# A sparse-attention loop: weighing and sum copy behind both pairs of heads of the next step

## What is computed

```
q, k, v = proj(Wq), proj(Wk), proj(Wv)         # 16 heads of 8, L = 1024, 32 blocks of 32
compressed_out = attn(q, mean of k per block, mean of v per block)
_, idx = top_k(block_scores, 8)                 # 8 blocks per head
selected_out = attn(q, k[idx], v[idx])          # the same 256 keys for all queries of a head
sliding_out  = attn(q, k, v, mask=(j <= i) & (j > i - 128))
out = g0 * compressed_out + g1 * selected_out + g2 * sliding_out
x = x + out @ Wo + bo
```

## Time and profile before

| what | value |
|---|---|
| time, median of three runs | 3937.93 us (3936.81 to 3938.05) |
| profiled execution, span | 3917.3 us, 87847 instructions |
| PE busy in the span | 3234.5 us (83%) |
| DVE busy | 2819.6 us (72%) |
| ACT busy | 2311.6 us (59%) |
| POOL busy | 1236.0 us (32%) |
| mean granted TensorE clock | 0.878 |

### The profile page before, as it was taken

One profiled execution on the slowest core, in us unless ns is written; L12 is line 12 of the kernel. 1 busy time (PEld: TensorE's weight loads), 2 busy tenths in 40 slices (PEclk: granted clock), 3 DMA queues, 4 the chain that ended last, 5 costly groups with the idle time before them and its releaser, 6 DMA issues. The chain is left out here.

```text
span 3917.3 us, 87847 instructions
## 1 busy us (share of the span) xinstructions
PE 3234.5 (83%) x36196; PEld 1484.2 (38%) x36256; DVE 2819.6 (72%) x4293; ACT 2311.6 (59%) x3868; POOL 1236.0 (32%) x1018
## 2 busy tenths in 40 slices
PE   6999999899867767699988888887995676776799
PEld 1222222266511121156533333333453554554445
DVE  8898899587679999887746667755535667656643
ACT  3888888766554555266532566665645564543565
POOL 1100100055537778545533000001004665452100
PEclk7999999899968788799999999998997676756799
DMA  4101010100010010100045011101000000000100
GB/s 102 28 9 28 20 21 5 37 2 2 11 32 17 17 33 17 35 15 2 13 71 76 10 38 32 27 21 53 1 9 3 4 4 4 4 4 3 31 7 17
DMA packets 136019, 84.34 MB, mean 22 GB/s; under 512 B 92386, under 2 KB 107539, under 8 KB 135491
## 3 DMA queue, kind: packets, MB, share of 16 engines
q1 hardware_dynamic: 132870, 74.45, 8.8%
q0 software_dynamic: 2688, 4.20, 0.7%
q10 hardware_dynamic: 64, 0.07, 0.0%
HBM read 46.97 MB, written 18.33 MB: 17 GB/s over the span
## 5 line engine op out<-in xcount | busy, mean ns | idle before, releaser
L993 DVE TENSOR_REDUCE attn_peak_halves<-attn_ps 128x2 f32<-128x1024 f32 x512 | 601.4, 1218 | 54.8 <-PE attn_ps L824 47.1
L946 ACT ACTIVATE attn_weights<-attn_ps 128x512 f32<-128x512 f32 x1024 | 531.1, 601 | 97.3 <-PE attn_ps L852 97.2
L2991 DVE TENSOR_REDUCE sparse_peak<-sparse_ps 128x4 f32<-128x1024 f32 x256 | 309.6, 1223 | 136.2 <-PE sparse_ps L2617 134.5
L1254 POOL TENSOR_TENSOR moe_hidden<-moe_exact,moe_hidden 128x512 f16<-128x512 f32 x256 | 296.7, 1163 | 331.9 <-ACT moe_hidden L1238 323.4
L3693 POOL TENSOR_TENSOR delta_q<-delta_q,delta_weighted 128x512 f32<-128x512 f32 x240 | 322.2, 1369 | 238.8 <-ACT delta_weighted L4087 238.7
L2844 ACT ACTIVATE sparse_weights<-sparse_ps 128x512 f32<-128x512 f32 (+1 forms) x512 | 272.0, 585 | 173.6 <-PE sparse_ps L2684 87.9
L250 PE MATMUL moe_ps<-moe_xT_halves,moe_w_halves 128*128 128x512 f16 x1536 | 364.0, 384 | 9.3 <-DVE moe_w_halves L1271 5.9
L1789 POOL TENSOR_TENSOR mamba_out_c<-mamba_states,mamba_c_rep 128x1024 f32<-128x1024 f32 x128 | 301.4, 2366 | 167.9 <-DVE mamba_states L1856 136.7
L852 PE MATMUL attn_ps<-attn_q_stack,attn_k_stack 50*128 50x512 f16 x1024 | 321.2, 385 | 27.0 <-ACT attn_weights L946 7.1
L250 PE MATMUL ffn_ps<-ffn_layers,ffn_h_halves 128*128 128x512 f16 x1536 | 334.5, 379 | 3.5 <-ACT ffn_gate L3236 3.5
L1575 PE MATMUL mamba_ps<-mamba_stack,mamba_spread 96*128 96x512 bf16 x512 | 194.0, 482 | 138.8 <-DVE mamba_states L1856 78.3
(11 more groups left out here) (450 smaller groups left out, 6280.9 us busy)
## 6 DMA issues: line engine op xcount, KB each, us to landing
mamba_stack<-mamba_parts SPq DMA_DIRECT2D x96, 128.0 KB, 2.4
sparse_factor<-sp_factor SPq DMA_DIRECT2D x24, 256.0 KB
sp_halves<-sparse_parts SPq DMA_DIRECT2D x8, 512.0 KB, 3.1
ffn_h<-in_h SPq DMA_DIRECT2D x4, 1024.0 KB, 7.8
attn_q_stack<-attn_halves SPq DMA_DIRECT2D x96, 32.0 KB
attn_k_stack<-attn_halves SPq DMA_DIRECT2D x96, 32.0 KB
attn_halves<-attn_hp SPq DMA_DIRECT2D x8, 384.0 KB, 3.1
attn_q_stack<-attn_peak_rows SPq DMA_DIRECT2D x128, 2.0 KB
```

What stands on the lines that cost most here:

```text
L946: act.activation(weights[:, at % 2, h, :], use.slot, ACT.Exp).then_inc(*key_act.one())
L993: dve.tensor_reduce(peak_halves[:, turn % PEAKS, keys, at:at + 2], use.slot, AX_X, ALU.max).then_inc(*score_dve.one())
L1254: pool.tensor_tensor(low, exact_sb[:, i % 3, :], hidden[:, i // EB % 3, i % EB, 0, :], ALU.subtract).then_inc(*hidden_low.one())
L2991: dve.tensor_reduce(peak[:, at % PEAKS, unit // 2, 4 * r:4 * r + 4], use.slot.rearrange("p h (a k) -> p (h a) k", a=2), AX_X, ALU.max).the ...
```

## The change

In each step the weighing of the step before stood between the first pair and the second, and the copy of its sum behind the second. Now both stand behind the second pair. The ten products of `warm` move with the weighing. Nothing else is changed: the calls are the same, and so is their number.

```diff
@@ -2215,10 +2215,11 @@
                             yield "exp", g, half, s, h
                         yield "pair", g, half, s, pair
                         yield from next_score()
-                        if g % GROUPS < 2 and n == 5 and pair == 0:
-                            yield ("warm", 10, *pending)
-                        if pending:
-                            yield ("sum" if pair else "weigh", *pending)
+                    if g % GROUPS < 2 and n == 5:
+                        yield ("warm", 10, *pending)
+                    if pending:
+                        yield ("weigh", *pending)
+                        yield ("sum", *pending)
                     pending = (g, half, s)
                     yield from between(g, n)
```

## The result

| | before | after |
|---|---|---|
| median, same chip (5 executions each) | 3937.93 us | 3915.49 us |
| lowest, highest | 3929.33, 3938.18 | 3910.77, 3920.11 |
| ratio | | 0.9949, 95% interval 0.9937 to 0.9962 |
| span of the profiled execution | 3917.3 | 3916.9 |
| its own time | not given | 3918.72 |

The change makes the kernel faster by 20 us (3937.93 x 0.0051), with an interval of 15 to 25.

What follows compares the result with a forecast made beforehand. Loop bound by a chain hopping between engines, mostly on TensorE. Terms 10.4 - 2 + 2.5 + 1 + 2 + 1 = 14.9 us take the span 3917.3 to 3902.4; plus 20.6, 3923, range 3908 to 3936.

Steps and rivals of the forecast that it cites:

- first steps: Loop's first steps: DVE's block scores hold TensorE up in some six places, the weighing moves into such waits; 1 us gained.
- numerators: Behind the second pair of s=1, seven times: they no longer hide an open exponential; 0.3 each, 2 us lost.
- last three halves: Halves without scores: 1.0 us saved at the wait for POOL, 2 us on six steps with a copy.
- Regular halves: Loop halves with scores: two take 25.92 us against 26.64, 0.36 saved a half, 10.4 us over 29 halves.
- open wait at s=1: Step s=1: the second pair waits for exponential 1 too, a new wait of 0.6 to 0.8 us.
- sign of being wrong: Regular steps s=3: the forecast is wrong if they do not shorten by some 0.15 us in the mean.
- Projections: Six in the loop: idle ahead falls from 2.4 to about 1.4 us, some may keep full clock; 2.5 us gained.
- Dummies: Ten dummy products of 8 steps: they stand before the weighing either way, their time is the same; costed at nothing.
- The 20.6: Whole kernel: timed median lies 20.6 us above the profiled span, for what is around it; carried over to the forecast.
- Waits only change place: Loop steps: later exponentials and 0.1 us longer handover per step take 11.6 of the 14.9 us back; 3935, chance 0.20.
- Slower, the clock falls at the wait of s=1: Loop halves: clock falls to 1.2 GHz once per half, 28 us net loss, 3966; slower cases together chance 0.09.
- The clock stays up: Projections and tail: the higher clock level holds after all of them; 24 to 28 us gained, 3912, chance 0.13.

Runs made afterwards that it cites:

- s3_only: Changed kernel, but weighing behind both pairs only in steps s=3, elsewhere and the dummies between the pairs as before; 3923.04 us, ratio 0.9966 to the kernel before.
- all_but_s3: Changed kernel, but in steps s=3 the weighing is between the pairs as before; 3934.63 us, ratio 1.0001 to the kernel before.
- before_filled: Kernel before the change with three dummy products added ahead of each of the six projections; 3933.86 us, ratio 0.9989 to the kernel before.
- s0_s3: Changed kernel, but weighing between the pairs at s=1 and s=2, behind both at s=0 and s=3, dummies between; 3896.14 us, ratio 0.9904 to the kernel before.
- warm_stays: Changed kernel with only the ten dummy products put back between the pairs; 3911.56 us, ratio 0.9940 to the kernel before.
- exit_swap: Changed kernel with the last half's inversion and factor store listed ahead of the previous half's projection after the loop; 3912.98 us, ratio 0.9947 to the kernel before.
- s1_back: Changed kernel with weighing and dummy products between the pairs again in steps s=1 only; 3898.78 us, ratio 0.9909 to the kernel before.
- before_again: The kernel before the change, unaltered, run and profiled once more; 3934.01 us, ratio 1.0002 to the kernel before.
- after_again: The changed kernel, unaltered, run and profiled once more; 3916.26 us, ratio 0.9948 to the kernel before.

## Why the prediction was right, and where it was not

My terms, put to the same four pieces (in us gained):

| piece | predicted | measured |
|---|---|---|
| first two halves: 0.7 of order, 1 of first steps | 1.7 | 1.4 |
| 27 halves: order 9.7, numerators -2, clock 2.5 | 10.2 | 10.1 |
| last three halves: 1 + 2 | 3 | 8.4 |
| exit | 0 | -2.9 |
| sum | 14.9 | 17.0 |

- **Regular halves, 25.92 for two.** Measured 25.98, so 0.33 a half and 8.9 for the 27. The waits for the copy went; the open wait at s=1 came at its place and in its size (0.6 to 0.8 said, 0.67 seen). s=1 is 3.35 (3.45 said), s=3 3.52 (3.48). One sign of being wrong was that the steps s=3 don't shorten by some 0.15 in the mean: they shorten by 0.12 (3.39 became 3.52 in a first half, 3.88 became 3.52 in a second), so the sign stands just short of its mark. s3_only shows that the move at s=3 brings the gain, as the prediction had it. That the cause is the wait for the copy is supported by 31 waits gone and not isolated: all_but_s3 has lost these waits too.
- **Numerators, 2 lost.** Their 384-wide step went from 4.79 to 4.92 where the plain one went from 3.30 to 3.20, 0.23 each; the 512-wide one went from 5.00 to 5.24 where the plain one went from 3.46 to 3.53, 0.17 each. That is 1.2 for the six in the 27 halves and 1.4 for all seven. Right.
- **Projections.** Idle 1.4 said, 1.43 and 1.64 found. The clock's term was 2.5. Set against the same steps at full clock (6.00, or 8.38 with dummies, in before_filled; 3.20 for the plain step behind), those of before were too long by 7.5 in sum. Those of after were too long by 4.4: twice 1.26 up to the second pair, and 0.90 and 0.96 in the step behind, whose dummies ran slower (6.69 and 6.75 instead of 5.79). So 3.1 was gained. before_filled, with the order of all else kept, gains 4.6 by three projections. Order 8.9, numerators -1.2, clock 3.1 and dummies -0.6 (2.26 instead of 2.17, seven times) make 10.2 of the measured 10.1.
- **Last three halves, 3.** This is the term that was mis-sized most. The scores run out two halves before the end, not three: DVE is busy 9.72 of the 13.65 us up to 2621.70 and 2.54 of the 35.9 behind. So 0.6 of the 8.4 is one more regular second half, and 7.8 is made in the last two. There TensorE's busy time fell by 5.2 (27.36 to 22.15), with the clock going from 0.76 to 1.00. Other kernels have three of the steps of before in the same order and at full clock. Two of them, before and then in s3_only, by their second pairs:
```profile
2644.95 0.61 PE L2664 MATMUL sparse_ps<-sparse_q_stack,sparse_p_stack 28*128 28x512 f16 x2
...
2651.47 0.39 PE L2684 MATMUL sparse_ps<-sparse_q_stack,sparse_k_stack 28*128 28x256 f16 x6
```
```profile
2633.38 0.39 PE L2670 MATMUL sparse_ps<-sparse_q_stack,sparse_p_stack 28*128 28x512 f16 x2
...
2637.93 0.39 PE L2690 MATMUL sparse_ps<-sparse_q_stack,sparse_k_stack 28*128 28x256 f16 x6
```
The step between them, which has numerators in it, took 6.52 before and 4.55 there; the step ahead of it 3.96 and 3.11; and the first step s=2 of the last two halves 4.74, and 3.02 in s0_s3. These three are 4.5 us of clock. The order and all else have at most 3.3 of the 7.8, and I had 3. I priced the order and forgot the clock, though the profile shows 0.76 there before. What raised it is open: warm_stays has the order of after there, and in it the lower level did come once (a step of 6.59 instead of 5.01).
- **Exit.** Not reckoned; 2.9 lost, shown by exit_swap. I followed the loop to its last pair and not the lists of the engines behind it.
- **Dummies, "at nothing".** Against before that is right within 0.7. But "their time is the same" (2.17 and 2.26 in fact) stopped the thought a step early: warm_stays shows 6.7 us that the new order offers and the change leaves. The same holds for the weighing at s=1, and that is worth more (s1_back).
- **The 20.6 "around the span".** Wrong: where an execution has both numbers 1.8 lie around it (3918.72 and 3916.9; 3930.63 and 3928.8 in before_again). The first profiled execution of before was quicker than any of the timed ones. The forecast is the median less the sum either way.

Two errors of opposite sign, 5.4 too little in the last halves and 2.9 of the exit not reckoned, leave 17.0 in the trace for 14.9 said; that these came so close is in part luck. At least 7.6 of the gain (3.1 and 4.5) is the clock, of which I had 2.5. The timed 20 has 15 to 25 as its interval, which holds 17.0; 14.9 lies at its lower edge.

**The rivals.** "Waits only change place" (3935) falls: the halves shortened in both profiles. "Slower, the clock falls at the wait of s=1" falls: the loop's clock is 0.98 with 0.67 of idle in every half. The Trainium skill (TensorE: Matmul & The Clock Gate, section "A second HAM failure mode: psum-queue depth-cycling") warns of such short idles between groups; the trace doesn't bear it out for 0.5 to 0.7 us, at a loop clock of 0.98. "The clock stays up" (3912, by 24 to 28 us) is half true, four of six projections and the last halves, and lies nearer to the timed 3915 than my forecast. It counted full gain at the projections and none of the loss at the exit.

## What to carry to other kernels

When filler work (a weighing, dummy products) is moved, ask for each step which wait it covers in the new place and which it uncovers: the distance between equal points of the cycle shows it, the sum of waits doesn't. Try the move per step: all four steps gave 20 us, two or three of them 35 to 41 (with and without the exit's order). Then read past the loop's end, since an engine's fixed list can put a ready operation behind one that still waits.

## What the runs showed of the hardware

- The length of the idle stretch alone doesn't decide the clock behind it. 1.43 us was followed by the lower level in none of 18 cases in six profiles. 1.64 was, at two of three in after, after_again and exit_swap, one of three in warm_stays, none of three in s1_back and s0_s3. 1.9 was at six of six in all_but_s3, but at two of six in before_filled, where dummies for 0.53 us followed. 2.4 was at five of six (before), 2.6 at two of three and 2.2 at two of three (s3_only), 2.0 at one of three (s0_s3). What else enters is open; before and after, each profiled twice, gave the same pattern both times.
- One spell at the lower level behind a projection cost 1.3 to 1.6 us in before and 2.2 in after, where it reached into the dummies of the next step.
- Single executions of the same kernel spread over 3924 to 3951 us on one chip, while its sparse stage repeats to 0.5: a stage's own length resolves what the kernel's time can't.
